# Start, gate and last joins of a batched two-branch block: five small moves between engines

## The reference

```python
# branch s: state-space mixer, then MLP
s = xn + mamba2(layernorm(xn, ln1))          # projections, 4-tap conv, chunked scan, gated rms, out_proj
s = s + gelu(layernorm(s, ln2) @ w1 + b1) @ w2 + b2
# branch f: 16-head causal attention with rms-normed q and k, then a top-2-of-4 mixture of experts
ao = attention(rms(xn)) @ wo ; ao[:, :, :32] = 0
f = xn + ao                                   # "x2": its first 32 columns are those of xn
moe = sum_e top2_weight_e(rms(f)) * expert_e(rms(f)) ; moe[:, :, :32] = 0
f = f + moe
out = x + s * silu(f)
```

## Time and profile before

| | |
|---|---|
| median of three runs | 847.98 us (847.05 to 848.3) |
| the profiled execution | 848.16 us; its span from the first to the last instruction is 846.4 us |
| PE busy | 777.2 us, 92% |
| DVE busy | 613.7 us, 73% |
| ACT busy | 510.2 us, 60% |
| POOL busy | 293.8 us, 35% |
| chain that ended last, by engine | PE 54%, DVE 18%, issue 12%, ACT 10%, POOL 4% |
| one round of the loop | 98.6 us |

### The profile page before, as it was taken

How to read it: one execution, slowest core, us unless ns; L and a number is a source line. 1 busy time by engine, 2 the same in 40 slices (tenths; PEclk the granted TensorE clock), 3 DMA queues, 4 the chain that set the end, 5 groups by cost and what they waited for, 6 DMA issues and landing times.

```text
span 846.4 us, 18186 instructions
## 1 busy us (share of the span) xinstructions
PE 777.2 (92%) x5482; PEld 486.3 (57%) x5482; DVE 613.7 (73%) x1491; ACT 510.2 (60%) x968; POOL 293.8 (35%) x577
## 2 busy tenths in 40 slices
PE   2779999999999999999899999999999999999997
PEld 1555564756547565665647565475556656475646
DVE  2685569785887868787697868878587877978624
ACT  2426784577753775467845677537754678456662
POOL 5413534143512616036240445216160262404400
PEclk9998999999999999999999999999999999999999
DMA  4000000000000000000000000000000000000000
GB/s 169 2 8 15 14 1 2 9 16 26 0 2 13 28 3 0 8 13 26 0 0 8 14 25 0 2 7 27 11 0 8 13 27 0 0 8 14 26 0 13
DMA packets 15145, 11.73 MB, mean 14 GB/s; under 512 B 1040, under 2 KB 13968, under 8 KB 14992
## 3 DMA queue, kind: packets, MB, share of 16 engines
q1 hardware_dynamic: 15120, 11.43, 4.5%
HBM read 7.76 MB, written 2.10 MB: 12 GB/s over the span
## 4 chain that ended last, share of the span: by engine, by line
PE 54%; DVE 18%; issue 12%; ACT 10%; POOL 4%; DVEq 1%; POOLq 0%; ACTq 0%
PE R L455 33%; PE S L455 13%; DVE sb_mx L1242 9%; ACT sb_pr L1136 3%; PE S L460 3%; DVE sb_cv L1260 2%; POOL sb_pr L1784 2%; PE R L573 2%; POOL sb_lnv L1680 2%; PE R L460 1%; DVE sb_x L1478 1%; ACT sb_junk L1053 1%; DVE sb_rqk L1387 1%; ACT sb_sq L1034 1%; PE R L616 1%
## 5 line engine op out<-in xcount | busy, mean ns | idle before, releaser
L1136 ACT ACTIVATE sb_pr<-S 128x768 f32<-128x768 f32 (+1 forms) x192 | 161.9, 886 | 111.8 <-PE S L455 111.8
L1242 DVE TENSOR_REDUCE sb_mx<-S 128x2 f32<-128x256 f32 (+3 forms) x256 | 198.0, 818 | 32.9 <-PE S L455 31.9
L1784 POOL TENSOR_SCALAR_AFFINE_SELECT sb_pr<-sb_pr 128x256 f32<-128x256 f32 (+1 forms) x192 | 98.7, 519 | 145.3 <-ACT sb_pr L1136 144.0
L455 PE MATMUL R<-sb_pr,sb_va 128*32 128x512 f32 (+3 forms) x1024 | 88.8, 441 | 3.4 <-POOL sb_pr L1784 1.2
L455 PE MATMUL R<-sb_W,sb_pr 128*128 128x96 f32 (+1 forms) x512 | 69.5, 276 | 0.0
L455 PE MATMUL R<-sb_xfT,sb_W 128*128 128x512 f32 x144 | 69.2, 602 | 0.0
L1771 POOL TENSOR_TENSOR sb_seg_r<-sb_seg_v,sb_seg_head 128x512 fp32r<-128x512 f32 x8 | 8.3, 1040 | 174.7 <-ACT sb_seg_v L1167 174.7
L455 PE MATMUL S<-sb_kT,sb_qT 32*128 32x256 f32 (+3 forms) x512 | 56.7, 385 | 13.0 <-DVE sb_mx L1242 10.2
L455 PEld LDWEIGHTS R<-sb_W,sb_pr 128*128 128x128 f32 x512 | 63.5, 192 | 3.8 <-issue 3.5
L455 PEld LDWEIGHTS S<-sb_kT,sb_qT 32*128 32x128 f32 x512 | 27.6, 183 | 65.5 <-DVE sb_mx L1242 58.2
L455 PE MATMUL S<-sb_qT,sb_kT 32*128 32x256 f32 (+3 forms) x512 | 56.5, 385 | 7.6 <-ACT sb_pr L1136 7.6
(11 more groups left out here) (230 smaller groups left out, 1726.1 us busy)
## 6 DMA issues: line engine op xcount, KB each, us to landing
sb_xin<-x SPq DMA_DIRECT2D x9, 256.0 KB, 2.8
sb_W<-weights SPq DMA_DIRECT2D x1, 2290.0 KB, 10.4
sb_qT<-sb_mT SPq DMA_DIRECT2D x128, 4.0 KB
sb_xres<-x SPq DMA_DIRECT2D x8, 256.0 KB, 2.8
out<-sb_xres SPq DMA_DIRECT2D x7, 256.0 KB, 2.3
sb_cT<-sb_xact SPq DMA_DIRECT2D x8, 128.0 KB, 2.3
sb_W<-weights SPq DMA_DIRECT2D x1, 514.0 KB, 4.6
sb_cst<-consts SPq DMA_DIRECT2D x1, 328.0 KB, 3.2
```

The source lines that it names most:

```text
L455: return pe.matmul(o, lhsT, rhs, start=start, stop=stop, skip_group_check=True)
L1136: act.activation(pr[:, e % 4, :, 0:n], S[pair_of_exp(e)][:, :, 0:n], ACT.Exp).then_inc(p_sb, 1)
L1242: o = dve.tensor_reduce(mx[:, n // P - 1, g, heads[0]:heads[1] + 1], found[:, :, at_col:at_col + n], AX.X, ALU.max, negate=True)
L1784: pool.affine_select(out=keep, in_=keep, compare_op=ALU.is_ge, fill=0.0, base=0, pattern=pattern, channel_multiplier=-1)\
```

## The change

Five edits:

1. POOL clears `xc`, `cs`, `cT` and `hst` behind the first norms and no longer ahead of them.
2. PE issues `dense(10)` as soon as the constants have landed, turns `xa`, issues `dense(2)`, and only then waits for the clears and tables.
3. The joins of the last batch for tiles 0 to 2 move from DVE to POOL; tile 3 stays on DVE. SP waits accordingly.
4. The copy of columns 0 to 31 of `x2` moves from DVE to POOL, to the start of POOL's stage B, with a semaphore of its own for ACT.
5. With a head, DVE runs only the first step of `gate_logits` ahead of the key copies and the other five behind the second of them; on ACT `gate_exp` moves from behind the second query copy to behind the third.

```diff
@@ SP, last batch
             for t in range(T):
-                sp_e.wait_ge(last_join, 2 * t + 2)
+                if t < T - 1:
+                    sp_e.wait_ge(pool_join, 2 * t + 2)
+                else:
+                    sp_e.wait_ge(last_join, 2)
                 sp_e.dma_start(out[B - 1, t * P:(t + 1) * P, :], xres[:, t, :]).then_inc(last_stored, 16)
@@ PE, ring_free
                 elif k == 3:
-                    pe.wait_ge(x2_sb, at(x2_sb, r, 2))
+                    pe.wait_ge(x2_sb, at(x2_sb, r, 1))
@@ PE, prologue
             pe.wait_ge(c_loaded, 48)
+            dense(R[0][:, 0:256], 10)
+            pe.wait_ge(xab_sb, at(xab_sb, -2, 1))
+            transposes(R[1], lambda t: xa[:, t, :]).then_inc(xaT_ps, 1)
+            dense(R[0][:, 0:256], 2)
             pe.wait_ge(pool_set, 11)
             pe.wait_ge(dve_set, 13)
-            pe.wait_ge(xab_sb, at(xab_sb, -2, 1))
-            transposes(R[1], lambda t: xa[:, t, :]).then_inc(xaT_ps, 1)
             pe.wait_ge(wh_loaded, 16)
@@ ACT, stage_b
                 if tail:
-                    act.wait_ge(x2_sb, at(x2_sb, r, 2))
+                    act.wait_ge(x2_sb, at(x2_sb, r, 1))
+                    act.wait_ge(x2m_sb, at(x2m_sb, r, 1))
                     act.wait_ge(yss_sb, at(yss_sb, r, 0))
...
                             act.activation(sp[:, 2], sp[:, 1], ACT.Exp, scale=-1.0).then_inc(spe_sb, 1)
-                            if tail:
-                                gate_exp(r)
+                        if tail and g == 2:
+                            gate_exp(r)
@@ DVE, stage_b
                     tt(x2[:, :, MASKED:D], R[3][:, 0:T * OC].rearrange("p (t c) -> p t c", t=T),
                        xn[:, :, MASKED:D], ALU.add).then_inc(x2_sb, 1)
-                    dve.tensor_copy(x2[:, :, 0:MASKED], xn[:, :, 0:MASKED]).then_inc(x2_sb, 1)
...
-                for _ in gate:
-                    pass
+                next(gate, None)
+                if not head:
+                    for _ in gate:
+                        pass
                 if head:
                     dve.wait_ge(e_ps, at(e_ps, r, 0))
                     for g in range(G):
                         dve.wait_ge(qkT_ps, at(qkT_ps, r, 2 * g + 2))
                         dve.tensor_copy(kT[:, g, :], bank((2 * g + 1) % 4)).then_inc(kT_sb, 1)
+                        if g == 1:
+                            for _ in gate:
+                                pass
@@ DVE, end
-            for t in range(T):
-                dve.wait_ge(last_silu, t + 1)
-                tt(gs[:, t, :], x1[:, t, :], gs[:, t, :], ALU.mult).then_inc(last_join, 1)
-                dve.wait_ge(last_join, 2 * t + 1)
-                tt(xres[:, t, :], gs[:, t, :], xres[:, t, :], ALU.add).then_inc(last_join, 1)
+            dve.wait_ge(last_silu, T)
+            tt(gs[:, T - 1, :], x1[:, T - 1, :], gs[:, T - 1, :], ALU.mult).then_inc(last_join, 1)
+            dve.wait_ge(last_join, 1)
+            tt(xres[:, T - 1, :], gs[:, T - 1, :], xres[:, T - 1, :], ALU.add).then_inc(last_join, 1)
@@ POOL, stage_b
+                if tail:
+                    pool.wait_ge(xn_sb, at(xn_sb, r, 0))
+                    pool.sem_inc(pool_passed, 1)
+                    pool.wait_ge(og_sb, at(og_sb, r, 0))
+                    pool.sem_inc(pool_passed, 1)
+                    ts(x2[:, :, 0:MASKED], xn[:, :, 0:MASKED], 1.0, 0.0, ALU.mult, ALU.add).then_inc(x2m_sb, 1)
@@ POOL, prologue
             pool.memset(tokqk[:], 0.0).then_inc(pool_set, 1)
+            for step in range(3):
+                first_norms(-2, step)
             pool.memset(xc[:, :, 0:3], 0.0).then_inc(pool_set, 1)
             pool.memset(cs[:], 0.0).then_inc(pool_set, 1)
             pool.memset(cT[:], 0.0).then_inc(pool_set, 1)
             pool.memset(hst[:], 0.0).then_inc(pool_set, 1)
-            for step in range(3):
-                first_norms(-2, step)
             pool.wait_ge(pool_set, 5)
@@ POOL, end
+            pool.wait_ge(sv_sb, at(sv_sb, B - 1, 1))
+            pool.sem_inc(pool_passed, 1)
+            pool.wait_ge(xres_loaded, at(xres_loaded, B - 1, 16))
+            pool.sem_inc(pool_passed, 1)
+            for t in range(T - 1):
+                pool.wait_ge(last_silu, t + 1)
+                tt(gs[:, t, :], x1[:, t, :], gs[:, t, :], ALU.mult).then_inc(pool_join, 1)
+                pool.wait_ge(pool_join, 2 * t + 1)
+                tt(xres[:, t, :], gs[:, t, :], xres[:, t, :], ALU.add).then_inc(pool_join, 1)
```

More of the change, by code:

```diff
@@ L248, in build @@
         last_join = signal("last_join", 0)
+        pool_join = signal("pool_join", 0)
         last_stored = signal("last_stored", 0)
@@ L332, in build @@
         ln2_sb = signal("ln2_sb", 2)
-        x2_sb = signal("x2_sb", 2)
+        x2_sb = signal("x2_sb", 1)
         nqk_sb = signal("nqk_sb", 3)
@@ L368, in build @@
         segr_sb = signal("segr_sb", 1)
+        x2m_sb = signal("x2m_sb", 1)
         pm_sb = signal("pm_sb", G * UNITS)
@@ L1799, in _ @@
                 pool.sem_inc(sem, per[sem.name])
-            for sem in (x1b_sb,):
+            for sem in (x1b_sb, x2m_sb):
                 pool.sem_inc(sem, per[sem.name])
```

## The result

The changed kernel is slower, by 0.4%: 851.28 us (849.5 to 853.42, 8 runs) against 847.93 us (847.05 to 850.01, 8 runs), ratio 1.0042 with a 95% interval of 1.0027 to 1.0056. I had forecast 843.5, and 842.0 to 846.0. The profiled execution took 852.05 us, 3.9 more than that of before.

| stretch | before | changed | difference |
|---|---|---|---|
| start to the turns of queries and keys of batch 0 on PE | 29.49 us | 26.15 us | -3.3 us |
| a loop round without a clock drop (line 1391, in the changed kernel line 1399, to itself) | 98.55 us | 99.75 us | +1.2 us, seven times |
| end of the last expert product on PE to the end of the last add on DVE | 3.53 us | 2.51 us | -1.0 us |

What follows compares the result with a forecast made beforehand. Bounds: POOL's clears and PE's lower clock in the prologue, ACT's first query copy in rounds, DVE's joins at the end. Prologue 3.5 plus joins 1.13 made 4.6 us off the profiled 848.16: 843.5 us, range 842.0 to 846.0.

Steps and rivals of the forecast that it cites:

- 1 and 2, prologue: Prologue: norms start 0.97 us earlier, turns save 0.44 and projection 2.28, less 0.20; sum 3.5 us.
- the first of my two cases: Prologue: PE's clock rises at 10.7, so unread products end at 12.65, before turns due at 13.03; otherwise 14.5.
- The 0.2 us that I took off for late rises of the clock: Prologue: deduction of 0.20 us for executions where PE's clock rises later during the unread products.
- Rival (a): Prologue: PE's clock does not hold until projection, or products outlast norms; 846.1 us, or 845.0 if only products late; chance 0.14.
- (e): Prologue: nothing won because something unseen is late next; only the end's 1.1 us remain, 847.0 us; chance 0.03.
- 3, joins: End: POOL joins tiles 0 to 2, so DVE's last add ends at 843.27 instead of 844.40, saving 1.13 us.
- Rival (b): End: POOL and DVE get in each other's way; one collision costs 0.49 us, giving 844.0 us; chance 0.10.
- 4, copy: Loop rounds: DVE's freed 0.22 us becomes longer waiting before line 1412; taken as 0, at most 1.5 us gained.
- 5, gate steps: Loop rounds: steps still take 0.89 us behind the second key copy; 0 to 0.4 us lost altogether, taken as 0.
- The slack that I had counted: Loop rounds: third key copy up to 0.22 us late, but the fourth by at most 0.06 us.
- The rule: Skill's statement that POOL and DVE share SBUF interfaces, with contention in two-port mode or with two SBUF inputs; forecast stayed 843.5.
- Rival (d): Loop rounds: all 0.89 us of gate steps fall on each round's path, costing 6.2 us; 849.7 us; chance 0.03.

Runs made afterwards that it cites:

- the kernel with POOL held: Changed kernel with POOL's addition of `b2` and convolution waiting for the third key copy in rounds with a head: 844.57 us, ratio 0.9951.

## Why the prediction was wrong

- **1 and 2, prologue: right.** 3.5 us predicted, 3.3 measured. The turns gave 0.44 us as predicted, the projection 2.1 instead of 2.28 (15.39 to 18.25), the clears 0.8 instead of 0.97: POOL began everything 0.16 us later, so that the first norm stood at 7.21, and DVE wrote `xa` in 1.27 us instead of 1.12 beside POOL's clears. The products ended at 13.2, half a microsecond later than the 12.65 of my sum (they started at 6.50 and not 6.3, and the slow ones took 0.43 us each, the first 0.56, and not 0.41). They just didn't delay the turns, so the first of my two cases held with nothing to spare; that is in part luck. The 0.2 us that I took off for late rises of the clock no run shows. Rival (a) is out, and so is (e).
- **3, joins: right**, 1.13 us predicted, 1.0 measured; DVE starts 0.1 us later behind the `silu` than I took. Rival (b) is out: the sums run undisturbed.
- **4, copy: right**, nothing.
- **5, gate steps: wrong, and this is the whole miss.** The failing step is "they follow the second key copy (end 221.90) and end at 221.90 + 0.03 + 0.89 = 222.82". I carried the 0.89 us of the old place to the new one. It was read where POOL ran only instructions of 0.2 to 0.3 us, and only the reduction started beside one; in the new place POOL is inside a row of instructions of 0.7 to 1.3 us, and the steps take 1.65. That turns "late by at most 0.06" into 0.5 us. The slack that I had counted (the third key copy may be 0.2 us late at no cost) was counted rightly, as the kernel with POOL held shows: there the move costs nothing (rounds of 98.52 us), and 4.1 us are won against the 4.5 that I forecast.
- **What I did not have at all** is the second meeting. Being late by half a microsecond made DVE's tap lose the start to a POOL add that it had beaten by 0.15 us, and that cost more than the lateness itself (0.73 against 0.47 us).
- **The rule was in hand.** I quoted it and asked it only of edits 3 and 4, whose instructions are new to POOL. It bears on every DVE instruction that is moved in time, and the stretched instruction of the earlier trace rows was the sign, as was the tensor_scalar of line 1359, stretched in every round of before. The Trainium skill, GPSIMD Engine Reference, section Specifications, names contention for DVE instructions in a two-port mode or with two SBUF inputs. For the second kind the traces agree, 0.63 us against 0.18. The tensor_scalars that were held have one input (1.27 and 0.50 us against 0.17); whether they ran in a two-port mode no run here shows.
- **Rival (d)** had the right place and the wrong mechanism, and with 3% far too little weight: it asked whether 0.89 us could fall on the path, not whether 0.89 would stay 0.89. Its threshold of 0.66 us a round was sound; the rounds lost 1.20.

## What to carry to other kernels

The duration of a small DVE instruction with two SBUF operands, or of a tensor_scalar, belongs to its place, not to the instruction: before moving one, lay POOL's timeline beside the new place and count each meeting as the rest of the POOL instruction that is running. Where an engine ends up a fraction of a microsecond late, look once more for what it then meets further on. And try moves one by one: four edits and ACT's half of the fifth, worth 4.8 us together (ratio 0.9944), became a loss of 3.4 us with DVE's half.

## What the runs showed of the hardware

- A DVE tensor_tensor of 128x16 with both operands in SBUF that starts while POOL runs is held to the end of POOL's instruction, also where that one has a single input (tensor_scalar, 0.77 us): 0.63 and 0.43 us instead of 0.17. It ends 0.02 to 0.04 us behind POOL, so what it costs is the rest of POOL's instruction and not its own size.
- A DVE tensor_scalar of 128x16 with a single input is held in the same way: 1.27 us in one round of the changed kernel and 0.50 us in the kernel before, instead of 0.17. A tensor_reduce beside a POOL instruction kept its 0.17 us, and sums with one operand in PSUM and one in SBUF took 1.37 us for four beside POOL and 1.38 without it.
- Who starts first wins, by little: the tensor_scalar of the gate took 0.16 us when it started 0.04 us ahead of POOL's instruction and 1.27 us when it started 0.02 us behind. With the tap first, DVE took its 0.74 us and POOL's instruction was stretched (1.09 instead of 0.69 us in the kernel with POOL held, 1.71 instead of 1.27 in the kernel before); started together with POOL's add, DVE took 1.81.
- With TensorE at its lower level in a prologue, unread work paid: 20 matmuls of constants in 6.85 us ahead of the turns brought the projection from 4.26 us (the kernel without them) to 2.82, and the split of the keys forward by 1.8 us. In the kernel before the projection took 4.95 us.
